# Graph layers and the LSTM of length one in common turns

## The reference, cut to what matters

```python
# layer 0
h = relu(einsum('ts,bsh->bth', adj, x @ Wg0 + bg0))
h = relu(einsum('ts,bsh->bth', adj, h @ Wg1 + bg1))
for p in range(1, 5):                       # windows of length p = 1, 2, 3, 4
    nw = 64 // p
    wins = h[:, :nw * p, :].reshape(128 * nw, p, 256)
    last = lstm_last(Wih[p-1], Whh[p-1], bih[p-1], bhh[p-1], wins)
    h = h.at[:, arange(nw) * p + (p - 1), :].set(last)
x = layernorm(x + h)
# layers 1 and 2: a graph convolution with batch norms, and edge attention
# layer 3 needs the eigenvectors of the graph's Laplacian
_, U = eigh(d_inv_sqrt[:, None] * (diag(deg) - adj) * d_inv_sqrt[None, :])   # 64 x 64
```

## Time and profile before

| | us |
|---|---|
| median of 3 runs (lowest, highest) | 2090.35 (2089.39, 2091.61) |
| the profiled execution | 2091.33 |
| its span, first to last instruction | 2089.5 |
| TensorE busy, share | 1948.3, 93% |
| VectorE busy, share | 1493.8, 71% |
| ScalarE busy, share | 1144.0, 55% |
| GpSimd busy, share | 758.3, 36% |

### The profile page before, as it was taken

The page is one execution under the profiler, slowest core; times in us unless marked ns, Lnnn a source line. Parts: engine busy times, 40 slices in busy tenths (PEclk is TensorE's granted clock), DMA queues, the critical chain, the costliest instruction groups (busy, mean ns, idle before and its releaser), DMA issues. The chain is left out here.

```text
span 2089.5 us, 32693 instructions
## 1 busy us (share of the span) xinstructions
PE 1948.3 (93%) x11833; PEld 1651.2 (79%) x11833; DVE 1493.8 (71%) x3825; ACT 1144.0 (55%) x1803; POOL 758.3 (36%) x1924
## 2 busy tenths in 40 slices
PE   6999888999999999999999989989799899699996
PEld 6999766788889999988787778866599534469896
DVE  5676666666656677788888878968656489789675
ACT  2444565445444454543444447747567588556675
POOL 2333345443444555000000036646544000107675
PEclk8999998999999999999999999999899999899898
DMA  3110101000100000010000033202222000004022
GB/s 107 47 41 1 41 1 41 1 1 1 41 1 1 1 1 1 1 41 1 1 1 0 1 106 102 91 21 92 69 82 72 11 1 1 11 21 123 32 71 82
DMA packets 65631, 71.15 MB, mean 34 GB/s; under 512 B 3767, under 2 KB 63294, under 8 KB 65470
## 3 DMA queue, kind: packets, MB, share of 16 engines
q1 hardware_dynamic: 65470, 69.07, 10.3%
HBM read 43.90 MB, written 25.17 MB: 33 GB/s over the span
## 5 line engine op out<-in xcount | busy, mean ns | idle before, releaser
L1852 ACT ACTIVATE l_gates<-l_acc,l_b 128x512 f32<-128x512 f32 (+1 forms) x504 | 300.9, 633 | 92.4 <-PE l_acc L473 90.0
L1859 ACT ACTIVATE l_gates<-l_cell 128x512 f32<-128x512 f32 (+1 forms) x144 | 84.0, 583 | 249.8 <-DVE l_cell L1913 156.3
L471 PE MATMUL l_acc<-l_x_hi,l_w1x_hi 128*128 128x336 f32 (+1 forms) x544 | 190.5, 350 | 20.4 <-DVE l_x_lo L1822 12.4
L1812 ACT ACTIVATE l_x_hi<-hT 128x512 fp32r<-128x512 f32 (+1 forms) x144 | 101.0, 755 | 172.4 <-PE l_acc L473 172.4
L473 PE MATMUL l_acc<-l_x_lo,l_w1x_hi 128*128 128x336 f32 (+1 forms) x544 | 190.5, 350 | 0.0
L472 PE MATMUL l_acc<-l_x_hi,l_w1x_lo 128*128 128x336 f32 (+1 forms) x544 | 190.2, 350 | 0.0
L471 PE MATMUL l_acc<-l_x_hi,l_w0x_hi 128*128 128x512 f32 x464 | 182.7, 394 | 6.7 <-ACT l_gates L1852 4.2
L472 PE MATMUL l_acc<-l_x_hi,l_w0x_lo 128*128 128x512 f32 x464 | 181.9, 392 | 0.0
L473 PE MATMUL l_acc<-l_x_lo,l_w0x_hi 128*128 128x512 f32 x464 | 181.8, 392 | 0.0
L183 POOL TENSOR_SCALAR bi_shifted<-bi_shifted 32x1 f32<-32x1 f32 x62 | 36.2, 585 | 400.1 <-DVE bi_shifted L173 400.1
L1243 ACT ACTIVATE leaky<-sc_g 128x1024 f32<-128x1024 f32 x128 | 121.1, 1031 | 21.8 <-PE sc_g L1357 21.4
(11 more groups left out here) (517 smaller groups left out, 6233.2 us busy)
## 6 DMA issues: line engine op xcount, KB each, us to landing
xin<-in_x SPq DMA_DIRECT2D x16, 512.0 KB, 3.9
hidB<-in_x SPq DMA_DIRECT2D x16, 512.0 KB, 4.9
x<-hT SPq DMA_DIRECT2D x16, 512.0 KB, 3.2
hidB<-x SPq DMA_DIRECT2D x16, 512.0 KB, 3.8
x<-hidB SPq DMA_DIRECT2D x16, 512.0 KB, 2.9
attention_residual<-x SPq DMA_DIRECT2D x16, 512.0 KB, 3.9
out_x<-hT SPq DMA_DIRECT2D x16, 512.0 KB, 2.9
l_rawx<-in_wih SPq DMA_DIRECT2D x4, 1024.0 KB, 5.0
```

Source lines behind the costliest of these rows:

```text
L471: t.matmul(out, left[0], right[0], start=start, stop=False)
L1812: i = nc.scalar.activation(as_windows(xs[s % 2][0][:, ch, 0:bg * nw], nw), cols(p, bg, nw, group, k, ch), ACT.Copy)
L1852: i = a.activation(gates[:, j, q, 0:n], acc[:, j, q, 0:n], FUNC[q], bias=b[:, o:o + 1])
L1859: a.activation(tcell[:, j, 0:n], cell[:, j, 0:n], TANH).then_inc(tc, 1)
```

## The change

The graph turns and the groups of length one become one sequence of 20 turns. Turn `it` does the first stages of group `it` and, `BEHIND` = 4 turns later, length one of that group: TensorE does second mix (group it - 2), unit 0 (group it - 4), first mix (it), second projection (it - 1), unit 1 (it - 4), first projection (it). All of it now shares the eight banks of `acc`: both mixes use banks 0 and 1 of the first half, both projections banks 2 and 3, and length one has the second half as a ring of four banks, each filled anew when its gate is read (`ring_read`). With that each mix waits until the other's result is copied out, and so does each projection. The reflections have fixed places (`REFLECTION_AT`): none in turns 0 and 1, one in turns 2 and 3, and two in each of turns 4 to 17, behind unit 0 and behind unit 1; that is 30 before length two, where it was 29. The weights of length one are loaded and split in turn 2, those of length two in turns 18 and 19. Length two's first products wait for all gates of length one. What later stages count of `gates_read` is smaller by the 32 units (`BEGIN`).

The diff, cut to its core:

```diff
-GRAPH_REFLECTIONS = GROUPS + 1
+BEHIND = 4
+
+REFLECTION_AT = {at: k for k, at in enumerate([(2, 0), (3, 0)] + [(it, half) for it in range(4, 18) for half in range(2)])}
...
-        ps_mix1, ps_h1 = ps("ps_mix1", [P, C, GROUP]), ps("ps_h1", [P, C, GROUP])
-        ps_pj, ps_mix2 = ps("ps_pj", [P, TILES, D]), ps("ps_mix2", [P, C, GROUP])
+        ps_mix, ps_h1 = acc[:, 0, 0:2, :], acc[:, 0, 2:4, :]
+        ps_pj = ps_h1.rearrange("p c (h d) -> p (c h) d", d=D)
+        ps_sums = acc[:, 1, 0, 0:P]
...
+            for it in range(1, TURNS):
+                g = it - BEHIND
+                if 0 <= it - 2 < GROUPS:
+                    rows_out(it - 2)
+                if g >= 0:
+                    lstm.gates(act, g, 0)
+                    lstm.tanh(act, g, 0)
+                if it < GROUPS:
+                    mixed_high(it)
+                if it - 1 < GROUPS:
+                    second_high(it - 1)
+                if it >= GROUPS + 2:
+                    lstm.weights_high(act, it - GROUPS - 2)
+                if g + 1 >= 0:
+                    lstm.rows_high(act, g + 1)
+                if g >= 0:
+                    lstm.gates(act, g, 1)
+                    lstm.tanh(act, g, 1)
+                if it < GROUPS:
+                    first_high(it)
+                if it + 1 < GROUPS:
+                    input_high(it + 1)
+                if it == 2:
                     act.wait_ge(l_in, 32)
                     a.activation(lw.split[0][:, :, :], lw.raw[:, :, :], ACT.Copy).then_inc(l_hi, 1)
-            for it in range(1, GROUPS + 3):
...
@@ in on_vector @@
+            for it in range(1, TURNS):
+                g = it - BEHIND
+                if it < GROUPS:
                     input_low(it)
-                if it >= 2:
-                    hh.back_update(v, it - 2)
-                    hh.front(v, dve, it - 1)
-                if 2 in stages:
-                    g = it - 2
-                    dve.wait_ge(pjh, g + 1)
-                    v.tensor_tensor(pj[1][:, :, :], ps_pj[:, :, :], pj[0][:, :, :].bitcast(F32), ALU.subtract).then_inc(pjl, 1)
-                if 1 in stages:
-                    g = it - 1
-                    dve.wait_ge(h1h, g + 1)
-                    v.scalar_tensor_tensor(h1[1][:, :, :], ps_h1[:, :, :], 0.0, h1[0][:, :, :].bitcast(F32),
-                                           ALU.max, ALU.subtract).then_inc(h1l, 1)
-                if 2 <= it <= GRAPH_REFLECTIONS:
-                    hh.back_products(v, dve, it - 1)
-                if 0 in stages:
+                reflection_products((it, 0))
+                if g >= 0:
+                    lstm.cell(dve, g, 0)
+                reflection_update((it, 0))
+                if g >= 0:
+                    lstm.hidden(dve, g, 0)
+                if it < GROUPS:
                     mixed_low(it)
+                if it - 1 < GROUPS:
...
@@ in on_tensor @@
+            for it in range(TURNS):
+                g = it - BEHIND
+                if 0 <= it - 2 < GROUPS:
+                    pe.wait_ge(pjl, it - 1)
+                    mix(pj).then_inc(m2, 1)
+                if g >= 0:
+                    lstm.products(pe, g, 0)
+                if it < GROUPS:
+                    pe.wait_ge(xl, it + 1)
+                    if it >= 2:
+                        pe.wait_ge(out, it - 1)
+                    elif it:
+                        pe.wait_ge(axl, it)
+                    mix(xs).then_inc(m1, 1)
+                if it == 1:
+                    pe.wait_ge(lo_w, 6)
+                    lap.row_of_scales(t, pe)
+                if 0 <= it - 1 < GROUPS:
+                    pe.wait_ge(h1l, it)
                     for r in range(TILES):
...
+                if g >= 0:
+                    lstm.products(pe, g, 1)
+                if it < GROUPS:
+                    pe.wait_ge(axl, it + 1)
+                    if it == 0:
                         pe.wait_ge(lo_w, 5)
-                        lap.row_of_scales(t, pe)
+                    else:
+                        pe.wait_ge(pjl, it)
...
             here = []
-            if p == 1 and group % 4 in (3, 0) and group:
-                here = [(u + 1, u + 1, update_last)]
-            elif p == 1 and group % 2 == 0:
-                here = [(u, u + 1, update_last)]
-            elif p in (2, 3) and k:
...
-                    for group in range(turns):
+                    for group in range(turns if p > 1 else 0):
...
+                if p == 2:
+                    pe.wait_ge(rows_done, GROUPS)
+                    pe.wait_ge(ring_read, 6 * GROUPS)
...
+        FIRST, RING = (0, 2, 3), 4
+        ring_read = sem("l_ring_read")
+
+        def ring(group, j, m):
+            return acc[:, 1, (6 * group + 3 * j + m) % RING]
+
+        def first_products(pe, group, j):
+            t, (xh, xl), x = nc.tensor, w[1][0], xs[group % 2]
+            if group == 0 and j == 0:
+                pe.wait_ge(first_done, 2)
+            if j == 0:
+                pe.wait_ge(x_lo, group + 1)
+            for m, q in enumerate(FIRST):
+                n = 6 * group + 3 * j + m
+                if n >= RING:
+                    pe.wait_ge(ring_read, n - RING + 1)
+                s = slice((2 * q + j) * P, (2 * q + j + 1) * P)
+                for ch in range(C):
+                    i = product(t, ring(group, j, m), (xh[:, ch, s], xl[:, ch, s]), (x[0][:, ch], x[1][:, ch]), ch == 0, ch == C - 1)
+                i.then_inc(x_used if (j, q) == LAST else gate_mm, 1)
+
+        def first_gates(act, group, j):
+            if group == 0 and j == 0:
+                act.wait_ge(first_done, 2)
+            else:
+                act.wait_ge(hd, 2 * group + j - 1)
+            for m, q in enumerate(FIRST):
+                if (j, q) == LAST:
+                    act.wait_ge(x_used, group + 1)
+                else:
+                    act.wait_ge(gate_mm, 5 * group + 3 * j + m + 1)
+                o = 2 * q + j
+                i = nc.scalar.activation(gates[:, j, q], ring(group, j, m), FUNC[q], bias=b[:, o:o + 1])
...
+        def first_cell(dve, group, j):
+            dve.wait_ge(ring_read, 6 * group + 3 * j + 2)
+            nc.vector.tensor_tensor(cell[:, j], gates[:, j, 0], gates[:, j, 2], ALU.mult).then_inc(cl, 1)
+
+        def first_hidden(dve, group, j):
+            p, bg, nw, _ = PLAN[0]
+            dve.wait_ge(ring_read, 6 * group + 3 * j + 3)
+            dve.wait_ge(tc, 2 * group + j + 1)
+            o3, t3 = (as_windows(z, nw) for z in (gates[:, j, 3], tcell[:, j]))
+            nc.vector.tensor_tensor(cols(p, bg, nw, group, 0, j), o3, t3, ALU.mult).then_inc(hd, 1)
+
```

More of the change, by code:

```diff
@@ L1574, in step, with on_tensor @@
                                     ALU.subtract).then_inc(l_lo, 1)
-            for it in range(1, GROUPS + 3):
-                if it == GROUPS + 2:
-                    lstm_input(0)
-                    lstm_input(1)
-                step(it, [s for s in range(4) if 0 <= it - s < GROUPS])
-        def on_tensor(pe):
+            lstm.rows_low(dve, GROUPS + 1)
+        def on_tensor(pe, lstm):
             t = nc.tensor
@@ L1627, in step, with __init__, lstm_layers @@
                     i.then_inc(p1, 1)
-                if 0 in stages:
-                    pe.wait_ge(xl, it + 1)
-                    mix(ps_mix1, xs).then_inc(m1, 1)
-            skewed(GROUPS, 3, step)
-        return (on_sync, on_gpsimd, on_scalar, on_vector, on_tensor), (out, l_lo)
-def lstm_layers(nc, sem, c, hT, wih, whh, first_weights, bi, hh, rows_done, first_done):
+        return (on_sync, on_gpsimd, on_scalar, on_vector, on_tensor), (out, l_lo, m2)
+class FirstWindows:
+    def __init__(self, **parts):
+        self.products, self.gates, self.tanh, self.cell, self.hidden = (parts[n] for n in (
+            "products", "gates", "tanh", "cell", "hidden"))
+        self.rows_high, self.rows_low, self.weights_high, self.weights_low = (parts[n] for n in (
+            "rows_high", "rows_low", "weights_high", "weights_low"))
+def lstm_layers(nc, sem, c, hT, acc, wih, whh, first_weights, bi, hh, rows_done, first_done, graph_done):
     with ExitStack() as ctx:
@@ L1706, in loops @@
                     split += turns * per_split
-                    if middle and not half:
+                    if middle and not half and p > 1:
                         middle(p)
@@ L1900, in body @@
                         ce = cell[:, j, 0:n]
-                        if p > 1 and unit in products:
+                        if unit in products:
                             hh.back_products(v, dve, products[unit])
@@ L1982, in _ @@
         def _(act):
-            graph[2](act, lambda s: rows_high(act, s))
+            graph[2](act, first)
             lstm[2](act, ahead[0])
@@ L1988, in _ @@
         def _(dve):
-            graph[3](dve, lambda s: rows_low(dve, s))
+            graph[3](dve, first)
             lstm[3](dve, ahead[1])
@@ L1994, in _ @@
         def _(pe):
-            graph[4](pe)
```

(1 more changed line is left out.)

214 lines of the change are left out of this document (115 added, 99 removed).

## The result

| | before | changed |
|---|---|---|
| median (lowest to highest), us | 2090.72 (2089.39 to 2091.61), 4 runs | 2124.45 (2118.17 to 2126.71), 4 runs |
| ratio, 95% interval | | 1.0157 (1.0135 to 1.0179) |
| profiled execution (span), us | 2091.33 (2089.5) | 2124.9 (2123.1) |
| first product with l_w0x (length two), us | 387.69 | 424.02 |
| from there to the end of the span, us | 1701.8 | 1699.1 |

The change is slower by 33.7 us. The direction was forecast, the size was not: 2105 was forecast, 14.7 above the median of that time. 36.3 us are lost before length two begins, and 2.7 come back behind it; 23.2 of the 36.3 are more waiting of TensorE, and the other 13 are its own work (363.0 us busy and not 349.9) at a lower mean clock, 0.93 and not 0.95.

What follows compares the result with a forecast made beforehand. Time before length two was taken to enter the total nearly one for one, with reflections bounding common turns at 22.4 us. Length two 17.6 later, minus 4.3, plus 1.7, gave +15.0: 2105 us, own range 2096 to 2115, full range 2077 to 2125.

Steps and rivals of the forecast that it cites:

- turn 4 begins: Start of the first turn with LSTM units: 77.6 us, after projections of turns 0 to 3 near 18, 36, 55, 74.
- first reflection of turn 4: Turn 4's first reflection on VectorE and GpSimd starts when input_low is through, near 81 us.
- thirteen turns: From turn 4's first reflection to turn 17's: 13 turns of 22.4 us, ending at 372.2 us.
- second front of turn 17 ends: VectorE's last front before length two ends a turn less one GpSimd piece after 372.2, at 388.3 us.
- from there to length two: Turn 18's cell, hidden, weight's low half (2.5), rows_low (1.2) and TensorE's last group (8.4): about 17 us.
- behind it: After length two begins: an old gap and slow stretch fall away (4.3 us), a new slow stretch costs 1.7.
- The common turns: Turns 4 to 17: two reflections a turn bound them at 22.4 us, 2.1 more than TensorE needs.
- the stretching: GpSimd's piece of a reflection loses 0.68 us per us of VectorE instructions with two SBUF inputs: pieces 7.3 and 6.3.
- rival 2: VectorE's SBUF pairs block GpSimd for every whole us: common turn 23.6 us, time 2122; chance 0.10.
- Rival 4: TensorE drops to 1.2 GHz in both waits of a common turn: turn some 24.3 us, time 2132; chance 0.07.
- Rival 1: GpSimd hardly stretched: two rings 19.8 us, under TensorE's 20.3 a common turn; time 2078; chance 0.17.

Runs made afterwards that it cites:

- first filling experiment: Unused matmuls put into TensorE's waits of turns 1 to 3, against the changed kernel (2124.45 us): 2116.68 us, one run.
- the early inputs: Next group's input copies ahead of the first projection's in turns 0 to 2, against a three-turns-behind kernel with 22 reflections before length two (2116.31 us): 2104.39 us, ratio 1.0060.

## Why the prediction was wrong, step by step

The working of the forecast and what the profile has, in us:

| step | forecast | measured | adds |
|---|---|---|---|
| turn 4 begins | 77.6 | 88.60 | 11.0 |
| first reflection of turn 4 | 81 | 92.12 | 0.1 |
| thirteen turns | 291.2 (22.4 each) | 296.3 (22.79 each) | 5.1 |
| second front of turn 17 ends | 388.3 | 404.02 | -0.5 |
| from there to length two | 17 | 20.0 | 3.0 |
| behind it | -2.6 | -2.7 | -0.1 |

The step that failed is "Worked through queue by queue, the projections of turns 0 to 3 begin near 18, 36, 55 and 74 us, and turn 4 at 77.6". The wait it names, for second_low, put at 2.6 us, is 2.46 in each turn. What it left out is TensorE's clock. It summed products at the price of full speed, while the same prediction charged 1.7 us for one slow stretch behind one wait of 2.57 us. With two waits a turn and no units between, the clock was 0.50 in four stretches, 10, 3, 7 and 10 us long (from 26.3, 40.0, 50.2 and 70.7 us), and each turn took 21 to 24 us, not 18 to 19. The waits were not what was missing: in the 68.3 us from turn 0's projection to turn 3's they are 17.7 us together, and the forecast's 56 us left at least 20 for them above TensorE's work (three turns of 11.92 at most). But TensorE's busy time is 50.6 us there. The first filling experiment shows that 7 of the 11 us come back with the clock, the early inputs that waits are in the way as well.

The common turns were right in mechanism and nearly right in size. VectorE waits at L204, twice a turn, 2.9 and 4.3 us, on GpSimd's L244; the pieces were 7.6 and 6.6 us, not 7.3 and 6.3. The term that was mis-sized is the stretching, "I take 0.68". In the changed kernel hidden, L1871 and the cell (0.61, 1.20 and 0.60 us by their starts) cost GpSimd 0.37 us in L183 and 1.78 in L189, 2.15 of 2.41, or 0.89 us per us, and input_low makes L186 1.67 us long and not 0.57: 1.10 for 1.20. The single instructions tell why the rows of before gave less: L183, caught by the lone hidden, loses 0.37 of 0.61 us, while L189, caught by L1871 and the cell in one run, loses 1.78 of 1.80. The first part of a run costs nothing where GpSimd is just at work or between two instructions; so many short runs, as before the change, cost a fraction, and one long run most or nearly all of it (the one of 2.50 us at 249.65 before cost L192 and L193 1.99; in turn 10 of the changed kernel L1871 and the cell, 1.99 us from 240.74 on, cost 1.40). This reading of the starts and ends is argued; no run varied it alone. I averaged over short runs and applied that to long ones. L192 alone, 1.54 of 1.87 us, had shown the lock. So the lock of rival 2, with 0.10, is what single instructions show, but not its price for the whole piece: it made the pieces 8.1 and 6.7 us. Its turn of 23.6 is near what turns 7 to 9 show (23.3 to 23.1) also because VectorE's own part of a reflection was 4.5 us there, not 4.38. The mean is lower since the reflections shrink as k grows (turns by L204 fall from 23.4 to 22.6) and since the last two, 21.0 and 20.6, have little or nothing beside their second piece, which the forecast charged in full. Rival 2's 2122 lies near the result, though its own turns are some 11 us too dear and the start it took from my sum 11 us too cheap.

The tail has two waits of 6.17 and 5.75 us on the rows' low halves, behind VectorE's last reflections and the weights' low half (2.29 us, 2.5 forecast), at a clock of 0.77 to 0.86; the forecast had one slow stretch there.

Rival 4 was right in another place than its own, and in its own it was nearly, not wholly, wrong: from 98 to 200 us the clock stayed at 1.00 behind waits of 1 to 1.4 us, but it fell to 0.50 twice in the thirteen turns, from 231.1 and from 299.4 us, with no longer waits ahead (1.22 and 1.01; 1.08 and 0.87). The ring wasn't delayed by it: the turns by L204 there are 22.6 us (from 233.34) and 22.7 (from 301.55), as their neighbours, and TensorE's next waits are shorter or missing instead. Rival 1 needed turns below 21.2, and they weren't. The waits for the copies out in the common turns go back to VectorE, held at L204, and not to ScalarE.

## What to carry to other kernels

When a stage is filled with a second job, cost the turns in which the second job isn't there yet with the clock that the waits leave, not with full speed. A ring between two engines that exceeds the turn by a tenth costs the whole gain of the overlap, and moving its parts to another stage only pays where that stage has room at that very place: look for the wait behind before counting the gain. When one engine's instructions are stretched by another's, compare start and end of single instructions; they show a lock, where averages over a piece show a fraction.
